# A graph network of two attention layers on one Trainium2 core: 13 instead of 16 projection products beside each unit of logits, 98 beside the scan, and logit parts added in TensorE

## The reference

```python
xp = (x @ W).reshape(N, 4, 256)                 # the projection of layer 0
e = leaky_relu((xp * att_src).sum(-1)[src] + (xp * att_dst).sum(-1)[dst], 0.2)
alpha = segment_softmax(e, dst)                 # self loops are added
x = layernorm(x + relu(segment_sum(xp[src] * alpha, dst) + bias))

h = rmsnorm(x) @ W_down                         # layer 1, 256 wide
msg = (h @ Wl)[src] + (h @ Wr)[dst]             # 4 heads of 64
e = (where(msg > 0, msg, 0.2 * msg) * att).sum(-1)
out = layernorm(x + segment_sum(segment_softmax(e, dst) * (h @ Wl)[src], dst) @ W_up)
```

## Time and profile before

| | value |
|---|---|
| profiled execution, its own time | 2091.52 us |
| its span | 2089.8 us |
| mean granted TensorE clock | 0.962 |
| TensorE busy | 1760.7 us (84%) |
| VectorE busy | 1598.7 us (76%) |
| ScalarE busy | 1177.3 us (56%) |
| GpSimd busy | 1059.9 us (51%) |

### The profile page before, as it was taken

The page is one execution under the profiler, slowest core; times in us unless marked ns, Lnnn a source line. Parts: engine busy times, 40 slices in busy tenths (PEclk is TensorE's granted clock), DMA queues, the critical chain, the costliest instruction groups (busy, mean ns, idle before and its releaser), DMA issues. The chain is left out here.

```text
span 2089.8 us, 51362 instructions
## 1 busy us (share of the span) xinstructions
PE 1760.7 (84%) x12291; PEld 1136.4 (54%) x12291; DVE 1598.7 (76%) x4381; ACT 1177.3 (56%) x4251; POOL 1059.9 (51%) x1564
## 2 busy tenths in 40 slices
PE   4899999997788888888883989578888888888598
PEld 3555555543465666666662877345555555555443
DVE  6577777748566666666666999479999999999677
ACT  3200000023677777777774766148788877888766
POOL 1022222220777777777770111577777777775050
PEclk9999999998899999999997999899999999999699
DMA  8445444420899999999998998466666666664567
GB/s 333 130 107 108 108 108 108 108 63 21 308 358 359 359 357 359 357 359 355 364 353 259 326 324 265 142 177 165 162 163 163 165 160 162 168 166 109 104 216 260
DMA packets 209860, 456.51 MB, mean 218 GB/s; under 512 B 41915, under 2 KB 111288, under 8 KB 209648
## 3 DMA queue, kind: packets, MB, share of 16 engines
q0 software_dynamic: 90000, 281.90, 39.6%
q1 hardware_dynamic: 89008, 144.64, 23.0%
q10 hardware_dynamic: 30672, 27.93, 6.4%
HBM read 419.97 MB, written 47.44 MB: 224 GB/s over the span
## 5 line engine op out<-in xcount | busy, mean ns | idle before, releaser
L161 POOL DMA_INDIRECT ring<-xl_table,isrc x440 | 446.6, 1015 | 151.4 <-issue 89.9
L1270 ACT ACTIVATE wone<-onehot,w 128x64 f32<-128x64 f32 x1760 | 432.3, 334 | 147.8 <-DVE onehot L1316 141.8
L1287 PE MATMUL banks<-w_sb,wone 128*64 128x256 f32 x2368 | 317.0, 393 | 78.9 <-DMA w_sb<-xp_table,isrc 48.5
L995 PE MATMUL banks<-w_sb,acc 128*128 128x512 f32 x736 | 342.3, 604 | 0.0
L161 POOL DMA_INDIRECT w_sb<-xp_table,isrc x296 | 295.5, 998 | 90.6 <-issue 46.3
L1843 ACT ACTIVATE w<-ring,pw 128x64 f32<-128x64 f32 x1320 | 325.5, 334 | 0.0
L1312 DVE TENSOR_TENSOR acc<-banks,acc 128x512 f32 x440 | 304.3, 692 | 0.0
L1890 PE MATMUL banks<-ring,ident 128*128 128x260 f32 x880 | 256.9, 415 | 0.0
L1287 PEld LDWEIGHTS banks<-w_sb,wone 128*64 128x64 f32 x2368 | 162.3, 137 | 129.0 <-issue 43.9
L1311 DVE TENSOR_TENSOR zacc<-banks,zacc 64x9 f32 x440 | 69.6, 158 | 186.5 <-PE banks L1290 170.5
L931 ACT ACTIVATE zacc<-pidx 128x450 f32<-128x450 f32 x1 | 0.6, 578 | 361.9 <-DVE onehot_t L1081 361.9
(11 more groups left out here) (343 smaller groups left out, 2874.0 us busy)
## 6 DMA issues: line engine op xcount, KB each, us to landing
acc<-xr_table SPq DMA_DIRECT2D x440, 66.0 KB
lt_bc<-local_dst ACTq DMA_DIRECT2D x110, 128.0 KB, 3.8
w<-acc SPq DMA_DIRECT2D x100, 128.0 KB, 4.5
x_table<-y POOLq DMA_DIRECT2D x25, 512.0 KB, 7.4
acc<-x_table SPq DMA_DIRECT2D x25, 512.0 KB, 3.6
low_bc<-src_low ACTq DMA_DIRECT2D x98, 128.0 KB, 4.3
acc<-in_x SPq DMA_DIRECT2D x12, 1024.0 KB, 13.8
xp_table<-xp_st SPq DMA_DIRECT2D x24, 512.0 KB
```

The costliest lines, as they stand in the source:

```text
L161: return self.pool.indirect_dma_start(out, None, table, bass.IndirectOffsetOnAxis(ap=idx, axis=0), bounds_check=self.bound, oob_is_err=False)
L995: last = nc.tensor.matmul(psum[:, 2 * r + i], xT_all[:, u, k, :], w_sb[:, k, i * 512:(i + 1) * 512], start=(k == 0), stop=(k == KD - 1))
L1270: last = nc.scalar.activation(wone[:, s, j, h, :], onehot[:, s, j, :], ACT.Copy, scale=w9[:, bass.ds(g * U + j, 1), h:h + 1].rearrange("p ...
L1287: nc.tensor.matmul(psum[WN * a:WN * (a + 1), j, k * C:(k + 1) * C], wone[:, s, j, h, :], slots[r][:, j, h * C:(h + 1) * C], start=True, st ...
```

## The change

Of the 384 products of tiles 1 to 24, 286 are now spread over the units, 3, 2, 3, 2 and 3 per group, as one stream that crosses tile borders (`products(count)`), and 98 stand in the scan (before: 352 and 32). Tiles 1 to 17 are complete within the units. Their evictions follow the table `EVICT_AT`, two turns behind the group that completes a tile, and VectorE's units are written out where they were a loop. The evictions of tiles 18 to 24 stand between VectorE's steps of the scan. `KEPT` is 8 instead of 12. ScalarE clears 10 tiles as soon as 18 tiles are projected, and 8 at the end of its program instead of 4. Six products of tile 24 come behind the last `weights_back`.

In the fused stage `finish` is taken out. `reduce` writes to a buffer `part` that holds three units, and the transpose of the first half of the logits becomes two products with the identity that accumulate in PSUM, one of `lg` and one of `part`. `product` writes its two pairs of tiles interleaved, so that `part` has the order of the edges.

```diff
-            KEPT = 12
+            KEPT = 8
+            HALVES = 2 * KD
+            SHARE = (3, 2, 3, 2, 3)
+            STREAM = [sum(SHARE) * (g // GU) + sum(SHARE[:g % GU + 1]) for g in range(NG)]
+            WHOLE = STREAM[-1] // HALVES
+            EVICT_AT = {1: 0, **{min(g for g in range(NG) if STREAM[g] >= HALVES * t) + 2: t for t in range(1, WHOLE + 1)}}
...
-                    act.wait_ge(s_xp, NU)
-                    for t in [*range(KEPT), *range(KEPT + 8, NU)]:
+                    act.wait_ge(s_xp, WHOLE + 1)
+                    for t in [*range(KEPT), *range(KEPT + 8, WHOLE + 1)]:
...
                         clear(acc[:, KEPT + i, :])
+                    act.wait_ge(s_xp, NU)
+                    for t in range(WHOLE + 1, NU):
+                        clear(acc[:, t, :])
...
-                    def halves(u, r, n0, n1):
-                        if n0 == 0:
-                            wait(pe, s_xe, u - 1)
-                        for n in range(n0, n1):
-                            k, i = divmod(n, 2)
-                            if isinstance(u, int) and u == NT - 1:
+                    streamed = itertools.count()
+
+                    def products(count):
+                        for n in itertools.islice(streamed, count):
+                            u, (k, i) = 1 + n // HALVES, divmod(n % HALVES, 2)
+                            if n % HALVES == 0:
+                                wait(pe, s_xe, u - 1)
+                            if u == NT - 1:
                                 last = nc.tensor.matmul(
-                                    psum[WN * i:WN * (i + 1), 2 * r], xT_all[:, u, k, 0:WN],
+                                    psum[WN * i:WN * (i + 1), 2 * (u % 2)], xT_all[:, u, k, 0:WN],
                                     w_sb[:, k, i * 512:(i + 1) * 512], start=(k == 0), stop=(k == KD - 1))
-                                continue
-                            last = nc.tensor.matmul(
-                                psum[:, 2 * r + i], xT_all[:, u, k, :],
-                                w_sb[:, k, i * 512:(i + 1) * 512], start=(k == 0), stop=(k == KD - 1))
-                        if n1 == 2 * KD:
-                            last.then_inc(s_xp, 1)
-
-                    def products(u, r, k0, k1):
-                        halves(u, r, 2 * k0, 2 * k1)
+                            else:
+                                last = nc.tensor.matmul(
+                                    psum[:, 2 * (u % 2) + i], xT_all[:, u, k, :],
+                                    w_sb[:, k, i * 512:(i + 1) * 512], start=(k == 0), stop=(k == KD - 1))
+                            if n % HALVES == HALVES - 1:
+                                last.then_inc(s_xp, 1)
 
...
-                    SLICES = ((0, 3), (3, 6), (6, 9), (9, 12), (12, 16))
-
                     def unit(u, r, static):
-                        for i, (n0, n1) in enumerate(SLICES):
+                        for i in range(GU):
                             look_up(GU * u + i, i, (GU * r + i) % 2)
                             if GU * static + i < NGC:
                                 look_up_sources(GU * u + i, (GU * r + i) % 2)
-                            halves(u + 1, 1 - r, n0, n1)
+                            products(SHARE[i])
                     for u in range(NU):
                         unit(u, u % 2, u)
 
-                    products(23, 1, 0, 2)
+                    products(16)
                     pe.wait_ge(s_lg, NG)
                     for b in range(NB):
                         for h in range(H):
                             last = nc.tensor.transpose(psum[0:TB, 4 + b, h * P:(h + 1) * P],
                                                        w9[:, b * TB:(b + 1) * TB, h], ident[:])
                         last.then_inc(scan["t1"], 1)
-                    products(23, 1, 2, 3)
+                    products(6)
                     for b in range(NB):
                         pe.wait_ge(s_vd, b + 1)
                         for h in range(H):
                             last = nc.tensor.transpose(psum[0:TB, 4 + b, h * P:(h + 1) * P],
                                                        w9[:, b * TB:(b + 1) * TB, H + h], ident[:])
                         last.then_inc(s_ts, 1)
-                    products(23, 1, 3, 6)
+                    products(28)
                     pe.wait_ge(scan["f1"], 1)
                     pe.wait_ge(scan["sv"], NB)
                     for b in range(NB):
                         nc.tensor.transpose(psum[0:H, 4, b * TB:(b + 1) * TB], fw[:, b, :, P - 1], ident[0:TB, 0:TB])
                         last = nc.tensor.transpose(psum[0:H, 5, b * TB:(b + 1) * TB], bw[:, b, :, 0], ident[0:TB, 0:TB])
                     last.then_inc(scan["t2"], 1)
-                    products(23, 1, 6, 7)
+                    products(4)
                     pe.wait_ge(scan["c"], 1)
                     for b in range(NB):
                         nc.tensor.transpose(psum[0:TB, 6, b * H:(b + 1) * H], cf[:, b * TB:(b + 1) * TB], ident[0:H, 0:H])
                         last = nc.tensor.transpose(psum[0:TB, 6, (NB + b) * H:(NB + b + 1) * H],
                                                    cb[:, b * TB + 1:(b + 1) * TB + 1], ident[0:H, 0:H])
                     last.then_inc(scan["t3"], 1)
-                    products(23, 1, 7, 8)
 
...
-                    products(24, 0, 0, 2)
+                    products(14)
                     weights_back(0)
-                    products(24, 0, 2, 4)
+                    products(8)
                     weights_back(1)
-                    products(24, 0, 4, 6)
+                    products(8)
                     weights_back(2)
-                    products(24, 0, 6, 8)
+                    products(8)
                     weights_back(3)
+                    products(HALVES * (NT - 1) - STREAM[-1] - 92)
 
...
-                    def evict_xp(u, r, m):
-                        if isinstance(u, int) and u == 0:
+                    def evict_xp(u):
+                        r = u % 2
+                        if u == 0:
                             dve.wait_ge(s_bias, 16)
                         dve.wait_ge(s_xp, u + 1)
-                        wait(dve, s_xs[r], 16 * m)
+                        wait(dve, s_xs[r], 16 * (u // 2))
                         nc.vector.tensor_tensor(xp_st[:, r], psum[:, 2 * r:2 * r + 2].rearrange("p a b -> p (a b)"),
...
-                        m = u // 2 if isinstance(u, int) else None
                         for i in range(GU):
                             turn(u, r, i, static)
-                            if i == 1:
-                                evict_xp(u, r, LOOP[0] if m is None else m)
-                    LOOP = [None]
-                    for u in range(2):
-                        unit(u, u, u)
-                    with dve.Fori(1, PICK_UNITS // 2) as pair:
-                        LOOP[0] = pair
-                        for r in range(2):
-                            unit(2 * pair + r, r, 2)
-                    for u in range(2 * (PICK_UNITS // 2), NU):
+                            if GU * u + i in EVICT_AT:
+                                evict_xp(EVICT_AT[GU * u + i])
+                    for u in range(NU):
                         unit(u, u % 2, u)
                     for i in range(LAG + 1):
                         turn(NU, NU % 2, i, NU)
-                        if i == 1:
-                            evict_xp(NU, NU % 2, NU // 2)
+                    evict_xp(WHOLE + 1)
 
...
                                                 bc(pen[:, b, :].unsqueeze(1), [TB, H, P]), ALU.add).then_inc(s_vd, 1)
+                    evict_xp(WHOLE + 2)
                     for b in range(NB):
                         dve.wait_ge(s_vd, b + 1)
+                        if b == 2:
+                            evict_xp(WHOLE + 3)
                         for h in range(H):
...
                                                  ALU.add, ALU.max).then_inc(scan["c"], 1)
+                    evict_xp(WHOLE + 4)
                     dve.wait_ge(scan["f1"], 1)
...
                             shift(b - 2, back[b - 2])
-                    evict_xp(23, 1, 11)
+                        if b == 3:
+                            evict_xp(WHOLE + 5)
+                    evict_xp(WHOLE + 6)
                     first_weights(0)
                     dve.wait_ge(scan["m"], NB)
...
-            part = sb("part6", [P, U, H])
+            part = sb("part6", [P, 3, H, BG, U])
...
-                    sp.wait_ge(s_lg, NG)
+                    sp.wait_ge(s_pt, NG)
+                    sp.wait_ge(s_sc, 2 * NG)
...
                         if i == 0:
-                            pe.wait_ge(s_lg, BG * u)
+                            pe.wait_ge(s_sc, 2 * BG * u)
+                            pe.wait_ge(s_pt, BG * u)
                             wait(pe, s_m, u - 1)
                             wait(pe, s_wv, u - 1)
                             if k == 1:
```

(37 more changed lines are left out.)

## The result

The kernel after takes **2077.0 us** (median, 2074.2 to 2082.2) where the kernel before takes 2090.8 (2087.0 to 2093.1): a ratio of 0.9933, 95% interval 0.9918 to 0.9948. It is faster, by 13.8 us or 0.7%. The profiled execution took 2076.9 us with a span of 2075.2.

A forecast was written before the change was run, and what follows sets the result against it. TensorE was taken to bound the units, VectorE to be fullest in the fused stage; 2091.5 - 12.4 (front) - 0.5 (fused stage) = 2078.6, called 2078 us against the median, range 2066 to 2086.

The forecast's parts named there:

- the front: Units and scan of the first layer together: -56.8 + 44.4 = -12.4 us.
- Units: Logits and projection units: 66 products fewer, 14.7 us a unit with TensorE still the bound, 56.8 us less.
- Z: The end of the units, at 473.9 us before; the scan's marks are forecast as distances from it.
- Rival 4: Units: VectorE's waits don't shrink, a unit takes 16.2 us, kernel 2111 us; decided from 15.3 us a unit; chance 0.06.
- Scan: First layer's scan: takes the moved products and grows from 50.5 to 94.9 us, by 44.4 us.
- Who ends it: End of the scan: ScalarE's eight clears finish at Z + 94.2, after SyncE at Z + 91.1; next block at Z + 94.9.
- rival 1: End of the scan: ScalarE's clears don't hold up the block, 3.1 us better, 2075 us; chance 0.10.
- Fused stage: Removing finish gives 0.00 us in the 100 turns with adds, -0.5 us in the first 10 turns.
- Rival 2: Fused stage: the removed slot is real, 0.30 us a turn, limited by GpSimd to some 19 us, 2059 us; chance 0.08.
- Identity products: Fused stage, TensorE: a unit's work grows by 0.3 us, hidden under 1.27 us of idle; without that cover 7 us.
- rival 3: Identity products, or the scan's slow clock, are not hidden: +7 us, 2085 us; chance 0.07.
- The small terms: Fused stage -0.5 us from its first 10 turns; preparation of the second layer 0.

The follow-up runs named there:

- the run with early clears: Changed kernel with four of ScalarE's last eight clears (tiles 18 to 21) moved ahead of its third copy of weights: 2075.3 us, ratio 0.9922 to the kernel before.
- the two mends above: Changed kernel with four of ScalarE's clears moved earlier and first_weights(0) ahead of tile 23's eviction: ratio 0.9949 to the kernel before, in a run with slow gathers.
- the best kernel here: Changed kernel with both mends in the front, plus one-hots and weighing placed between the fused stage's adds: 2045.5 us, ratio 0.9767 to the kernel before.

## Why the prediction was right

The prediction was 2078 us, the median is 2077.0, and each large term has its counterpart in the trace. That the total is within 1 us is partly luck: the front came out 1.6 us better than forecast in the profiles, and two stages that scatter by 2 us moved against each other.

1. **Units.** Predicted 56.8 us less, with TensorE full at 14.7 us a unit: measured 14.74, and Z moved by 57.2, of which 0.6 lie ahead of the units. That VectorE, at 13.1 to 13.2 us, isn't the bound is confirmed down to 13.87 us a unit by the run with 12 products. Rival 4, with units over 15.3 us, is out.
2. **Scan.** Predicted to grow by 44.4 us, measured 93.7 - 50.5 = 43.2. The marks, as distances from Z: VectorE's mid-scan wait 9.25 us (about 9), carries copied at 55.5 (56.0), third `weights_back` at 79.6 (80.0) behind a wait of 1.25 (about 1), last product at 87.7 (88.6), SyncE through at 90.4 (91.1), clears done at 93.4 (94.2), memset at 93.7 (94.9). Two terms were mis-sized: a product of tile 24 takes 0.45 us (16 instructions in 3.65) and not 0.49, since the row that I took it from covers only four of them, with the step to the transposes in it (its granted clock was 1.00, so the clock isn't why); and the block opens 0.26 us behind ScalarE, not 0.65. I had taken 0.65 from an end on SyncE's queue, and behind SyncE it is 0.65 again in the run with early clears. The two together are some 1.0 of the 1.2 us.
3. **Who ends it.** ScalarE's clears (2.7 us when half of them are moved), then the chain through the third `weights_back` (1.3 us more): both as forecast, and rival 1 is wrong.
4. **Fused stage.** Predicted 0.00 us in 100 turns, measured nothing (1.0001, 0.9989 to 1.0013) with this part alone. The sequence after, an add 0.22 us idle behind an add, is that of the earlier trace rows; 93 such waits stand in the stage. Rival 2, the slot as real time, is wrong for the removal and right for the gap: nothing is won by emptying it, 27.2 us by putting work in.

   The Trainium skill's advice to minimize the number of operations rather than semaphores ("VectorE: DVE Perf Modes", Rules for kernel authors) gained nothing on these adds: one operation less a turn gave 0, while the same number in another order gave 0.25 us a turn. Its section "The DRAIN you can't avoid" measured a run of copies with and without a semaphore behind each and found that the semaphore costs nothing extra there. Two adds back to back start 0.51 us apart here for an instruction of 0.28; but an add has both a wait and a register address ahead of it, no run parts the two, and so the trace neither confirms nor refutes that sentence.
5. **Identity products.** Predicted +0.3 us a unit and hidden; measured +0.3, and hidden (rival 3 out), while four pairs cost 17 to 18 us.

The small terms came out by cancelling. The fused stage was 2.3 us shorter where I had 0.5 (with the old fused stage it was 1.9 shorter in the run with the new front alone), and the preparation of the second layer 1.8 us longer where I had 0. That preparation took 215.1 to 216.0 us in the three kernels with the old front and 214.1 to 218.9 in seven with the new one and usual gathers, among which nothing in it differs, so I read it as scatter; it wasn't tested.

## What to carry to other kernels

When an engine is full in one stage and idle in the next, move work by the piece, price it from rows at full clock, and write the receiving stage out as distances from one mark: all the small waits then have a place, and the two mends above were read off that list. Ask of an instruction what the next one would wait for without it: between two dependent instructions it may be free, and taking it out is then worth nothing, while independent work moved into such gaps is worth all of them. Extra work hidden under an idle time of 1.3 us has a size at which it is no longer hidden; when a full engine is relieved, as in the best kernel here, count again who is next.

## What the runs showed of the hardware

- An add on VectorE that waits for the add before it and takes its address from a register starts 0.22 us behind that add's end, 93 times in the stage after. An add of the same form starts 0.29 us behind the start of a 0.19 us instruction that it doesn't depend on. So the gap isn't an idle time behind every instruction; whether the wait or the register work makes it wasn't tried.
- A block opened 0.26 us behind the end of ScalarE's last activation (after, and with 12 and with 14 products) and 0.65 us behind the end of SyncE's last issue (before, and with early clears), whichever came last.
- TensorE's granted clock: 0.87 in the scan with idle times of 2.8 and 7.8 us, 1.00 when its longest idle time there was 1.25 us. In the run with 14 products it was 0.90 from 490 to 512 us, behind the idle time of 4 us.
- The same 440 tiles of gathers took 585 to 588 us in ten kernels' profiles and 727 to 728 us in four, with the same chip number on both sides: gather times are compared only among runs made together.
